# Where the odd slot of a pair of attention steps stands among TensorE's instructions

## The chip, the cores and the metric

The kernel runs on one core of a Trainium2 chip. The metric is device time in microseconds (us): the median of three executions of the kernel before is 1056.26 us (1056.03 to 1058.4).

## What is computed

A perceiver block: cross-attention of 256 latent rows over 4096 context rows (batch 4, width 256, 16 heads of 16), then a causal linear attention over the latents with exponential features, then a gated feed-forward. Each is added to `x` after a layer norm. Cut to what matters:

```python
Q = layernorm(x) @ Wq.T + bq; K = ctx @ Wk.T + bk; V = ctx @ Wv.T + bv     # per head: 16 columns
x = x + softmax(Q K^T / 4) V @ Wh.T + bh                                   # 256 x 4096 scores, 16 heads, 4 batches
qf, kf = exp(clip(norm(q) @ omega*sqrt(2s) - s)); A = causal(qf kf^T)      # the linear attention, per head
x = x + (A v / (A 1)) @ Wout + bout
x = x + (silu(h @ wg.T) * (h @ wu.T)) @ wd.T                               # h = layernorm(x), integer weights
```

## The kernel before, in words

The context of a batch is cut into 8 chunks of 512 rows; the loop calls them passes, p0 to p7. A pass has 16 steps. One step is 128 context rows (one of four tiles) times 4 heads. Its scores are 4 matmuls into one of the two score tiles `ps_s` (line 711), ScalarE takes their exponential into one of four `probs` tiles (line 975), and its values product is 4 fp32 matmuls (8 instructions) of 17 columns each, side by side in four column strips of the array, added up in `ps_o` (line 700). The values product lags its scores by two steps.

While a pass attends, TensorE also projects the chunks to come, through the one bank `ps_p`: the values of the next chunk, tile 0 to 3, in steps 1, 3, 5 and 7 (V0 to V3, line 546, 6 matmuls), and the keys of the chunk after it in steps 9 and 12 (K0 and K1, line 538, 6 matmuls). Most of these steps are odd. VectorE takes each result out of `ps_p` (V: line 1034; K: lines 1012 to 1019), and the next projection waits for that (`v_ready`, `k_out`).

Everything else of the block is spread over the steps of a later batch as named stages. A tail stage belongs to the batch before (`oT0`, `wh`, `ln1T`, `feat0` to `feat7`, `A0` to `A15`, `pv0` to `pv3`, `gu0` to `gu5`, `down` and so on), a head stage to the batch after (`ln0`, `ln0T`, `q`, `kbd`, `max0` to `max3`, `maxT`). Batches are counted 0 to 3: batch 0 carries only head stages, batches 1 and 2 both, batch 3 only tail stages, and the tail of batch 3 runs alone at the end. The table `AT` gives a tail stage its step, `HEAD_AT` a head stage. All products of stages go through the one bank `ps_a`, so `stage` on TensorE waits until VectorE has finished the stage whose product stood there before (`ready`, semaphore `operand`). Some stages (`ln0`, `kbd`, `o`, `gate0` to `gate5`) are on VectorE alone.

What a step carries beside its attention (a projection and the stages that fall on it) is its slot. `fast_slot(b, p, s)` on TensorE issues the slot's projection first and then its stages. VectorE has a `fast_slot` of its own that takes the same things in the same order, slot by slot. One wait there matters below: before V0 of a pass is copied to its buffer (`fast_values_out`), VectorE waits until all values products that read that buffer are done (`pv_done`); the last two of them are issued in steps 0 and 1 of the same pass.

TensorE handles two steps at a time (a pair: s even, s + 1). Written S for the two steps' scores (8 matmuls), E for the even slot, O for the two values products of the pair before (16 instructions), D for the odd slot, a pair is S E O D. The score tile of a step is free again when the exponential of the step two before has been taken.

Of the kernel before, what the change touches and what calls it, by code (L numbers as in the profile page):

```python
# [209 lines left out]
def perceiver(nc, x, ctxT, wqT, bq, wkT, bk, wvT, bv, whT, bh, wqkv, bqkv, wout, bout,  # L210
              omega, nodes, weights, wgT, wuT, wdT, out):
    ctx = ExitStack()
    with ctx:
# [116 lines left out]
        def head_of(b):  # L330
            return (b, b - 1, False)
# [4 lines left out]
        def stages_at(b, step):  # L336

            return [(n, tail_of(of) if n in TAIL else head_of(of)) for of, n in stages_of(b, step)]
# [188 lines left out]
        def _(pe):  # L527
# [22 lines left out]
            def project_keys(c, q, j):  # L550

                pe.wait_ge(c["ctx_split"], q + 1)
                if j:
                    pe.wait_ge(c["k_out"], q * 2 + 1)
                elif q:
                    pe.wait_ge(c["v_ready"], q * TT)
                for part in range(CI):
                    project(c, ("k", j, part), q, q % 2)

            def project_values(c, q, tile):  # L560

                if tile:
                    pe.wait_ge(c["v_ready"], q * TT + tile)
                else:
                    pe.wait_ge(c["k_out"], q * 2 + 2)
                project(c, ("v", tile, 0), q, q % 2)
# [117 lines left out]
            def products(c, names, clock, alone=False):  # L684
                for name in names:
                    if alone and name[:4] == "gate" and name != "gate0":

                        down_part(c, int(name[4:]) - 1, ps_a, clock)
                    if name not in VECTOR_ONLY:
                        stage(c, name, clock, alone)  # L690
# [43 lines left out]
            def fast_scores(b, q, s):  # L734

                n = q * STEPS + s
                if n >= LAG:
                    pe.wait_ge(fast["exp_done"], n - LAG + 1)
                score(fast, s, q % 2, qstacks[b % 2])

            def fast_values(n):

                b, q, s = n // BS, n // STEPS, n % STEPS
                if b and n % BS == 0:
                    pe.wait_ge(fast["operand"], fast.at("operand", tail_of(b - 1), "o"))
                value_product(fast, n, s, q % 2, q % NCH == 0, q % NCH == NCH - 1, q * TT + s // G)

            def fast_slot(b, p, s):

                q = b * NCH + p  # L750
                if s in VALUE_SLOTS and q + 1 < B * NCH:
                    project_values(fast, q + 1, VALUE_SLOTS[s])
                if s in KEY_SLOTS and q + 2 < B * NCH:
                    project_keys(fast, q + 2, KEY_SLOTS[s])
                for name, clock in stages_at(b, p * STEPS + s):
                    products(fast, [name], clock)
# [19 lines left out]
            for b in range(B):  # L776
                for p in range(NCH):
                    q = b * NCH + p
                    if p == 0:
                        pe.wait_ge(fast["q_stacked"], (b + 1) * Q_STACKED)  # L780
                        pe.wait_ge(fast["operand"], fast.at("operand", head_of(b), "maxT"))
                    if p == 0 and b == 1:
                        pe.wait_ge(late_in, 16 * 15)
                        pe.wait_ge(w_ready, 1)
                    pe.wait_ge(fast["k_stacked"][p % 2], (q // 2 + 1) * STACKED)
                    for s in range(0, STEPS, LAG):
                        for t in range(LAG):
                            fast_scores(b, q, s + t)
                        fast_slot(b, p, s)
                        if q or s:  # L790
                            for t in range(LAG):
                                fast_values(q * STEPS + s + t - LAG)
                        fast_slot(b, p, s + 1)
            for t in range(LAG):
                fast_values(B * BS + t - LAG)
            products(fast, TAIL[:NORMALISED], tail_of(B - 1), True)
# [597 lines left out]
```

## Time and profile before

| | |
|---|---|
| median of 3 executions | 1056.26 us |
| the profiled execution | 1058.43 us, its span 1056.3 us |
| TensorE matmul busy | 943.5 us, 89% of the span |
| VectorE, ScalarE, GpSimd busy | 566.0, 548.6, 113.6 us |
| first scores | 45.4 us |
| batch 0, 1, 2, 3 of the loop | from 45.4, 238.4, 479.0, 721.4 us; the loop ends at about 935 us |
| last tail, alone | about 935 to 1056.3 us |

The matmul rows of a trace are pipelined: a matmul is listed as longer than the distance to the next one. The distance between the starts of two rows tells what a piece of the order costs, and so the start of a pair's first score matmul to that of the next pair is the length of a pair. A batch has 64 pairs. "Idle before <- releaser" names the last event that an instruction waited for.

### The profile page before, as it was taken

To read this page: it belongs to the slowest core of one execution; us is meant where nothing else is said; L and a number is where in the kernel's file an instruction comes from. 1 tells how busy PE (TensorE), PEld (TensorE's weight loads), DVE (VectorE), ACT (ScalarE), POOL (GpSimd) and SP (SyncE) were. 2 spreads that over 40 slices of the span, in tenths; PEclk is the share of its full clock that TensorE was granted. 3 is DMA by queue.
4 is the path that set the end of the run, shared out by engine and by line. 5 is a ranking of instruction groups with operands and counts; after the bars stand their busy time and mean duration, and the time that the engine had idled before them with its cause. 6 is when DMAs were issued, how large, how long until landed. Compare 5 with 4: busy or idle time off the path is not lost.

```text
span 1056.3 us, 20657 instructions
## 1 busy us (share of the span) xinstructions
PE 943.5 (89%) x8586; PEld 621.2 (59%) x8595; DVE 566.0 (54%) x1009; ACT 548.6 (52%) x595; POOL 113.6 (11%) x137
## 2 busy tenths in 40 slices
PE   4689999999999998799999998979999999955765
PEld 3456665656666665566666765556566666632544
DVE  7633335565555457745654557645555556514546
ACT  5157666667466555446465555536565655820101
POOL 1700000000311100000221000000131100003300
PEclk9799999999999999999999999989999999986887
DMA  4997665587555555257655554266655543110000
GB/s 137 212 216 137 136 130 110 120 159 158 105 111 96 110 110 111 65 91 143 132 107 111 110 106 96 65 110 138 123 110 111 102 90 72 30 41 0 1 1 12
DMA packets 65219, 108.94 MB, mean 103 GB/s; under 512 B 21537, under 2 KB 52641, under 8 KB 61665
## 3 DMA queue, kind: packets, MB, share of 16 engines
q1 hardware_dynamic: 63328, 103.17, 47.6%
q0 software_dynamic: 1792, 4.40, 1.7%
q8 instruction: 70, 1.15, 0.5%
q14 instruction: 29, 0.23, 0.1%
HBM read 78.71 MB, written 28.84 MB: 102 GB/s over the span
## 4 chain that ended last, share of the span: by engine, by line
PE 68%; DVE 12%; issue 7%; ACT 4%; DMA 4%; POOL 2%; DVEq 2%; SPq 0%; POOLq 0%
PE ps_o L700 17%; PE ps_s L711 17%; PE ps_p L546 9%; PE ps_p L538 9%; ACT probs L975 4%; DVE kfeat L1207 2%; PE ps_a L654 2%; PE ps_a L680 2%; PE ps_a L648 2%; PE ps_a L593 2%; DMA kstack<-kscr 2%; PE ps_a L667 1%; PE ps_a L637 1%; POOL rnorm L878 1%; PE ps_a L655 1%
## 5 line engine op out<-in xcount | busy, mean ns | idle before, releaser
L975 ACT ACTIVATE probs<-ps_s 128x1024 f32<-128x1024 f32 x512 | 497.2, 1022 | 384.3 <-PE ps_s L711 383.3
L711 PE MATMUL ps_s<-qstack,kstack 128*128 128x256 bf16 x2048 | 277.0, 276 | 24.1 <-DVE ksample L1116 8.8
L700 PE MATMUL ps_o<-probs,values 128*17 128x256 f32 x4096 | 274.9, 385 | 0.0
L711 PEld LDWEIGHTS ps_s<-qstack,kstack 128*128 128x128 bf16 x2048 | 184.3, 99 | 93.2 <-issue 43.0
L700 PEld LDWEIGHTS ps_o<-probs,values 128*17 128x17 f32 x4096 | 96.2, 97 | 109.9 <-issue 38.9
L1034 DVE TENSOR_TENSOR values<-ps_p,bv_sb 128x256 f32<-128x256 f32 x128 | 54.2, 423 | 145.1 <-PE ps_p L546 145.0
L1012 DVE TENSOR_SCALAR kparts<-ps_p,b_heads 128x512 bf16<-128x512 f32 x64 | 48.1, 751 | 102.1 <-PE ps_p L538 101.8
L546 PE MATMUL ps_p<-wv_hi,ctx_hi 128*128 128x256 f32 x256 | 86.8, 339 | 10.7 <-DVE values L1034 5.8
L546 PEld LDWEIGHTS ps_p<-wv_hi,ctx_hi 128*128 128x128 f32 x256 | 49.2, 192 | 66.2 <-issue 50.2
L546 PE MATMUL ps_p<-wv_hi,ctx_lo 128*128 128x256 f32 x256 | 73.1, 285 | 0.0
L546 PE MATMUL ps_p<-wv_lo,ctx_hi 128*128 128x256 f32 x256 | 72.9, 285 | 0.0
L538 PE MATMUL ps_p<-ctx_hi,wk_hi 128*128 128x512 f32 x128 | 57.6, 450 | 7.9 <-DVE values L1034 3.5
L881 POOL TENSOR_TENSOR rstd<-veps,half_power 128x2 f32<-128x2 f32 x12 | 8.4, 696 | 507.2 <-DVE veps L1047 507.2
L911 POOL TENSOR_TENSOR kfeat<-feat,half_mask 128x256 f32<-128x256 f32 x64 | 37.9, 613 | 227.8 <-ACT feat L952 227.8
L952 ACT ACTIVATE feat<-feat,node_neg 128x512 f32<-128x512 f32 x32 | 23.1, 722 | 68.7 <-DVE feat L1191 68.7
L538 PE MATMUL ps_p<-ctx_hi,wk_lo 128*128 128x512 f32 x128 | 51.6, 403 | 0.0
L538 PE MATMUL ps_p<-ctx_lo,wk_hi 128*128 128x512 f32 x128 | 51.4, 401 | 0.0
L1014 DVE SCALAR_TENSOR_TENSOR krest<-ps_p,b_heads,kparts 128x512 f32<-128x512 f32 x64 | 48.1, 751 | 5.1 <-issue 0.4
L546 PEld LDWEIGHTS ps_p<-wv_hi,ctx_lo 128*128 128x128 f32 x256 | 49.7, 194 | 0.0
L546 PEld LDWEIGHTS ps_p<-wv_lo,ctx_hi 128*128 128x128 f32 x256 | 49.5, 193 | 0.0
L878 POOL TENSOR_TENSOR rnorm<-ss,half_power 128x32 f32<-128x32 f32 x8 | 43.9, 5502 | 38.1 <-DVE ss L1178 38.1
L1019 DVE TENSOR_TENSOR kparts<-krest,kparts 128x512 bf16<-128x512 f32 x64 | 44.3, 692 | 5.6 <-issue 0.9
(214 smaller groups left out, 998.7 us busy)
## 6 DMA issues: line engine op xcount, KB each, us to landing
kscr<-kparts SPq DMA_DIRECT2D x64, 384.0 KB, 2.6
kstack<-kscr SPq DMA_DIRECT2D x32, 768.0 KB, 7.8
ctx_raw<-ctxT SPq DMA_DIRECT2D x32, 512.0 KB, 13.2
kstack<-kscr SPq DMA_DIRECT2D x32, 512.0 KB, 10.4
kstack<-kscr SPq DMA_DIRECT2D x32, 256.0 KB, 11.7
qstack<-qscr SPq DMA_DIRECT2D x16, 128.0 KB, 4.4
qscr<-qparts SPq DMA_DIRECT2D x4, 384.0 KB, 3.3
xh<-x SPq DMA_DIRECT2D x4, 256.0 KB, 13.6
```

What stands on the lines that cost most here:

```text
L538: last = mm(ps_p[:, :], w[:, k, j * P:(j + 1) * P], a[:, k, :], start=(k == 0 and n == 0), stop=(k == CI - 1 and n == 2))
L546: last = mm(ps_p[:, 0:D], a[:, k, j * P:(j + 1) * P], w[:, k, :], start=(k == 0 and n == 0), stop=(k == CI - 1 and n == 2))
L700: last = mm(ps_o[32 * j:32 * j + DH + 1, g * S:(g + 1) * S], values[par][:, i, g * GH + j, :], probs[s % NPROB][:, j * S:(j + 1) * S], sta ...
L711: last = mm(ps_s[s % 2][:, j * S:(j + 1) * S], kstack[par][:, u, i * P:(i + 1) * P], queries[:, u, :], start=True, stop=True)
L878: pool.tensor_tensor(rnorm[:, n, :], ss[:, n, :], half_power[:, n, :], ALU.pow).then_inc(c["powered"], 1)
L911: pool.tensor_tensor(kfeat[:, p % 2, k, :], feat[:, p % 2, 1, :], half_mask[:, k:k + 1].to_broadcast([P, S]), ALU.mult).then_inc(c["kfeat" ...
L952: nc.scalar.activation(feat[:, p % 2, :, :], feat[:, p % 2, :, :], ACT.Exp, bias=node_neg[:, :]).then_inc(c["acted"], 1)
L975: nc.scalar.activation(probs[n % NPROB][:, :], ps_s[n % 2][:, :], ACT.Exp, scale=float(DH) ** -0.5).then_inc(fast["exp_done"], 1)
L1012: v.tensor_scalar(kparts[:, 0, j, :], ps_p[:, :], bias, None, ALU.add)
L1014: v.scalar_tensor_tensor(krest[:, :], ps_p[:, :], bias, kparts[:, 0, j, :], ALU.add, ALU.subtract).then_inc(c["k_out"], 1)
L1019: v.tensor_tensor(kparts[:, 2, j, :], krest[:, :], kparts[:, 1, j, :], ALU.subtract).then_inc(c["k_parts"], 1)
L1034: v.tensor_tensor(values[q % 2][:, tile, :, 0:DH], ps_p[:, 0:D].rearrange("p (h d) -> p h d", h=H), bv_sb[:, :].rearrange("p (h d) -> p h ...
```

## The change

In the loop over pairs, TensorE issues the odd slot right behind the even one, ahead of the two values products. The pair S E O D becomes S E D O. Nothing is added or removed, and the lists of instructions of VectorE, ScalarE, GpSimd and the DMA queue stay as they are.

```diff
@@ -787,10 +787,10 @@
                         for t in range(LAG):
                             fast_scores(b, q, s + t)
                         fast_slot(b, p, s)
+                        fast_slot(b, p, s + 1)
                         if q or s:
                             for t in range(LAG):
                                 fast_values(q * STEPS + s + t - LAG)
-                        fast_slot(b, p, s + 1)
```

TensorE in batch 1, pass 3, steps 6 and 7, before. Line 655 ends stage `A4` (even slot), line 700 is the values product, line 546 is V3 and the last row begins stage `A5` (odd slot):

```order
L655 MATMUL ps_a<-feat,kfeat 128x128
L700 MATMUL ps_o<-probs,values 17x256 [waits f_v_ready,f_exp_done]
L700 MATMUL ps_o<-probs,values 17x256 x3
L700 MATMUL ps_o<-probs,values 17x256 [waits f_exp_done]
L700 MATMUL ps_o<-probs,values 17x256 x3
L546 MATMUL ps_p<-wv_hi,ctx_hi 128x256 [waits f_v_ready]
L546 MATMUL ps_p<-wv_hi,ctx_lo 128x256
L546 MATMUL ps_p<-wv_lo,ctx_hi 128x256
L546 MATMUL ps_p<-wv_hi,ctx_hi 128x256
L546 MATMUL ps_p<-wv_hi,ctx_lo 128x256
L546 MATMUL ps_p<-wv_lo,ctx_hi 128x256
L654 MATMUL ps_a<-feat,kfeat 128x256 [waits f_kfeat,f_operand]
```

The same place of TensorE now:

```order
L655 MATMUL ps_a<-feat,kfeat 128x128
L546 MATMUL ps_p<-wv_hi,ctx_hi 128x256 [waits f_v_ready]
L546 MATMUL ps_p<-wv_hi,ctx_lo 128x256
L546 MATMUL ps_p<-wv_lo,ctx_hi 128x256
L546 MATMUL ps_p<-wv_hi,ctx_hi 128x256
L546 MATMUL ps_p<-wv_hi,ctx_lo 128x256
L546 MATMUL ps_p<-wv_lo,ctx_hi 128x256
L654 MATMUL ps_a<-feat,kfeat 128x256 [waits f_kfeat,f_operand]
L655 MATMUL ps_a<-feat,kfeat 128x128
L700 MATMUL ps_o<-probs,values 17x256 [waits f_v_ready,f_exp_done]
L700 MATMUL ps_o<-probs,values 17x256 x3
L700 MATMUL ps_o<-probs,values 17x256 [waits f_exp_done]
```

Between the end of `A4` and the start of `A5`, which waits for VectorE's copy of `A4` (`f_operand`), there stood a values product and V3; now V3 alone stands there. The values product follows `A5`.

TensorE at the start of a pass (batch 1, pass 3, steps 0 and 1), before: the end of `feat2`, the values product, V0 (its first row waits for `f_k_out`), then `A2`:

```order
L648 MATMUL ps_a<-qkT,om_sb 128x256
L700 MATMUL ps_o<-probs,values 17x256 [waits f_exp_done]
L700 MATMUL ps_o<-probs,values 17x256 x3
L700 MATMUL ps_o<-probs,values 17x256 [waits f_exp_done]
L700 MATMUL ps_o<-probs,values 17x256 x3
L546 MATMUL ps_p<-wv_hi,ctx_hi 128x256 [waits f_k_out]
```

The same place of TensorE now, from V0's last matmul on:

```order
L546 MATMUL ps_p<-wv_lo,ctx_hi 128x256
L654 MATMUL ps_a<-feat,kfeat 128x256 [waits f_kfeat,f_operand]
L655 MATMUL ps_a<-feat,kfeat 128x128
L700 MATMUL ps_o<-probs,values 17x256 [waits f_exp_done]
L700 MATMUL ps_o<-probs,values 17x256 x3
L700 MATMUL ps_o<-probs,values 17x256 [waits f_exp_done]
L700 MATMUL ps_o<-probs,values 17x256 x3
```

VectorE at this place, before and now alike (the copies of `feat2`, V0, `A2` and `A3`, and V1):

```order
L1191 TENSOR_SCALAR feat<-ps_a,clip_most,clip_least 128x512 [waits f_product]
L1034 TENSOR_TENSOR values<-ps_p,bv_sb 128x16x16 [waits f_pv_done,f_v_proj]
L1195 TENSOR_TENSOR amat<-ps_a,causal 128x384 [waits f_product] x2
L1034 TENSOR_TENSOR values<-ps_p,bv_sb 128x16x16 [waits f_v_proj]
L1197 COPY qk<-ps_a 128x256 [waits f_product]
```

The values product that V0's copy waits for (`f_pv_done`) was issued before V0; now it is issued behind V0 and `A2`.

## Rows read from the trace of the kernel before

**Rows 1.** The page: busy time of each engine, its share, instructions.

```profile
PE 943.5 (89%) x8586; PEld 621.2 (59%) x8595; DVE 566.0 (54%) x1009; ACT 548.6 (52%) x595; POOL 113.6 (11%) x137
```

**Rows 2.** Batch 3: us; PE, PEld, DVE, ACT, POOL busy (count); PE clock, DMA share, GB/s.

```profile
721.40:935.00 213.60, 212.19 (x2063) 140.06 (x2060) 111.54 (x198) 131.44 (x147) 21.88 (x20) 1.00 0.46 97
```

**Rows 3.** Waits of PE in batch 1: us in total, times, longest.

```profile
PE ps_s L711 <- DVE ksample L1116: 4.1, 1, 4.1
PE ps_a L585 <- DVE amat L1201: 2.3, 1, 2.3
```

**Rows 4.** Timeline of PE, pairs with V3, K0, and K1: start, length, what.

```profile
128.04 1.05 PE L711 MATMUL ps_s<-qstack,kstack 128*128 128x256 bf16 x8
...
130.82 1.05 PE L711 MATMUL ps_s<-qstack,kstack 128*128 128x256 bf16 x8
...
134.30 1.05 PE L711 MATMUL ps_s<-qstack,kstack 128*128 128x256 bf16 x8
...
372.58 1.04 PE L711 MATMUL ps_s<-qstack,kstack 128*128 128x256 bf16 x8
...
375.94 0.61 PE L711 MATMUL ps_s<-qstack,kstack 128*128 128x256 bf16 x4
```

**Rows 5.** Timeline of PE, batch 1, pass 3, steps 6 and 7.

```profile
332.28 0.38 PE L655 MATMUL ps_a<-feat,kfeat 128*128 128x128 f32 x2
332.60 1.06 PE L700 MATMUL ps_o<-probs,values 128*17 128x256 f32 x16
333.59 0.38 PE L546 MATMUL ps_p<-wv_hi,ctx_hi 128*128 128x256 f32 x1
...
334.40 0.59 PE L654 MATMUL ps_a<-feat,kfeat 128*128 128x256 f32 x2
334.83 0.38 PE L655 MATMUL ps_a<-feat,kfeat 128*128 128x128 f32 x2
335.05 0.82 PE L711 MATMUL ps_s<-qstack,kstack 128*128 128x256 bf16 x6
```

**Rows 6.** Timeline of DVE at that place: the copy of A4.

```profile
332.70 0.56 DVE L1195 TENSOR_TENSOR amat<-ps_a,causal 128x384 f32<-128x384 f32 x1 [1.12 <-PE ps_a L655]
```

**Rows 7.** Timeline, batch 1, pass 4, steps 0 to 2: `feat5`, its copy, `A8`.

```profile
351.59 1.03 PE L648 MATMUL ps_a<-qkT,om_sb 128*128 128x256 f32 x4
352.65 0.81 DVE L1191 TENSOR_SCALAR feat<-ps_a,clip_most,clip_least 128x512 f32<-128x512 f32 x1 [0.44 <-PE ps_a L648]
...
353.52 0.70 PE L654 MATMUL ps_a<-feat,kfeat 128*128 128x256 f32 x2
```

**Rows 8.** Timeline, start of batch 2: the copy `o`, `oT0` and its copy.

```profile
481.37 1.23 DVE L1154 COPY qk<-ps_o 128x1024 f32<-128x1024 f32 x1
...
482.91 0.60 PE L624 MATMUL ps_a<-ident,qk 128*128 128x128 f32 x4
...
484.53 0.42 DVE L1072 TENSOR_TENSOR y<-ps_a,rden 128x256 f32<-128x256 f32 x1
```

**Rows 9.** Timeline, batch 1, pass 1: chain of `wh`, copy of V1, then V2.

```profile
268.12 0.69 DVE L1162 TENSOR_TENSOR xs<-xs,ps_a 128x512 f32<-128x512 f32 x1 [1.49 <-PE ps_a L593]
...
271.66 0.42 DVE L1034 TENSOR_TENSOR values<-ps_p,bv_sb 128x256 f32<-128x256 f32 x1
272.13 0.39 PE L546 MATMUL ps_p<-wv_hi,ctx_hi 128*128 128x256 f32 x1 [0.28 <-DVE values L1034]
```

**Rows 10.** PE in batch 1, pass 5: K0 behind the chain of `wout`.

```profile
397.69 0.47 PE L538 MATMUL ps_p<-ctx_hi,wk_hi 128*128 128x512 f32 x1 [0.37 <-DVE values L1034]
```

**Rows 11.** PE in batch 0, pass 5: V1 behind the set-up on DVE.

```profile
171.26 0.39 PE L546 MATMUL ps_p<-wv_hi,ctx_hi 128*128 128x256 f32 x1 [2.00 <-DVE values L1034]
```

**Rows 12.** DVE in batch 1: the copy of `gu0`; `kbd`.

```profile
408.23 0.42 DVE L1201 TENSOR_TENSOR amat<-kfeat,ps_a 128x256 f32<-128x256 f32 x1 [0.91 <-ACT kfeat L959]
...
446.98 1.29 DVE L1116 TENSOR_TENSOR ksample<-kparts,head_mask 128x512 bf16<-128x512 bf16 x2
```

**Rows 13.** The stretch behind `max0` in batch 1 (columns as in Rows 2).

```profile
448.50:453.10 4.60, 4.54 (x32) 2.89 (x31) 1.22 (x3) 2.60 (x4) 0.00 (x0) 0.63 1.22 189
```

## The prediction, as it was made

> **What bounds the kernel now.** I read the page first, then the waits of PE batch by batch, then the timeline of PE pair by pair. PE is busy for 89% of the span, the next engine for 54% [rows 1], and in the stretch of batch 3, where no head stages run, PE is busy for 212.2 of 213.6 us at full clock [rows 2]. So in the loop, 890 of the 1056 us, the time is the length of TensorE's list, pair after pair. Two things can lengthen or shorten it: what it costs to pass from one kind of matmul to the next, and waits, of which there are few now. In batch 1 the two largest are 4.1 us for `kbd` (it is `max0` that waits, its record is missing and the wait is booked on the next scores) and 2.3 us for `gu1`'s copy ahead of `ln0T` [rows 3]. The other engines keep their lists, so all that can change is when TensorE gets to its instructions.
>
> **Part 1, the seams get cheaper.** A pair with K0 in its odd slot (S O D) takes 134.30 - 130.82 = 3.48 us; a pair with K1 in its even slot, which already has the order S E O, takes 375.94 - 372.58 = 3.36 us [rows 4]. Same work, same clock: the order S D O is 0.12 us shorter than S O D. The V pair has the same two seams (128.04 to 130.82, 2.78 us [rows 4]); I take 0.11 us for both. There are 124 V's and 30 K0's in the loop, so this part is worth at most 154 x 0.11 = 17 us.
>
> By the Trainium skill (TensorEngine Tiling (Array Packing), Key Properties) changing the tiling mode, and not just the tile, drains TensorE. The values product is the only one in column strips beside `pv`, and a plain pair enters and leaves it once in either order, so by that rule alone this part would be worth nothing, and the sum below would come out some 12 us higher, 1085 us: slower still. The two rows of K pairs say 0.12 us; I go by them.
>
> **Part 2, the copies of neighbours are no longer covered.** All stages share one bank. Where the even and the odd slot of a pair both have a stage, the odd one waits for VectorE's copy of the even one. Before, a values product and a projection stood between; now the projection alone. From the last matmul of `A4` (the second of the x2 at 332.28, 0.11 us later) to `A5` at 334.40 there were 2.0 us [rows 5]; without the values product (332.60 to 333.59, 0.99 us) and with cheaper seams 0.82 us are left. What is needed is the product's end, the copy and its release:
> - `A`: last matmul 332.39, copy from 332.70 for 0.56 [rows 5, 6], release 0.06: 0.93 us. A stall of 0.11 cancels the saving of the seam: 0.0 for `A4`/`A5`, `A8`/`A9`, `A14`/`A15`. Where a `pv` follows (`A3`, `A11`) it then stands beside the values product with no change of strips between: I take -0.3 each, and for `pv1` and `pv3`, which stood beside it before and now don't, +0.3 each. Bounds for these four: from -0.3 to +0.5 each.
> - `feat`: last matmul 352.24 (351.59 and three of 0.216), copy from 352.65 for 0.81, next stage 353.52 [rows 7]: 1.28 us, a stall of 0.46, less the seam 0.1 and a little for the wider exit: +0.27, three times (`feat0`/`feat1`, `feat2`/`A2`, `feat6`/`A10`).
> - `oT0`/`oT1`: last matmul 483.23 (482.91 and three of 0.108), the copy's last part ends at 484.95 [rows 8]: 1.78 us, +0.87. `o2T1`/`y2T` has the same copy without the check of the denominators, some 0.4 us less: +0.45. `ln1T`/`qk0`, a plain copy: +0.15.
>
> Sum per tail: 0.8 + 0.9 + 0.45 + 0.15 = 2.3 us, thirteen neighbours.
>
> **Part 3, long chains that end in an odd slot.** After `wh` (even) VectorE has a layer norm from 268.12 on, only then copies V1 at 271.66, and V2 waits until 272.13 [rows 9]. V2's time is set by `wh`, not by what TensorE does between. Before, two values products ran ahead of V2, now one, and the second comes behind it: the wait grows from 0.35 us by a whole values product with its seams, 0.99 [rows 5] + 0.1, and the savings of V1 and V2 are lost in it. Net +1.1. K0 behind `wout` is the same [rows 10]: +1.1. In batches 1 and 2 `ln0T` and `max0` are such places as well: VectorE goes without a pause of note from the copy of `gu0` (408.23) to that of `gu1`, and from the copy of `gu4` to `kbd` at 446.98 [rows 3, 12]. Also once V1 behind the set-up in batch 0 [rows 11], and in batch 0 `ln0T` and `max0`, which wait there too. Each +1.1. If such a chain's start came earlier by as much as the values product, it would be 0; each is bounded by 0 and +1.3.
>
> **Part 4, V0's copy waits for the values product behind it.** VectorE stops at V0's copy until that product is done, then takes V0's copy (0.42) and that of the odd stage in the same slot. From `A2`'s last matmul: product 0.88, its release 0.37, V0 0.42, copy 0.56, release, 2.35 us with the gaps between, against 2.07 us until `A3` asks: +0.3. With the copies' lengths of the others: `yT`/`wh` +0.4, `feat5`/`A8` +0.5, `A15`/`pv3` +0.15. Per tail +1.35. In the plain passes only V1 could wait, 0.26 us are spare, so nothing. In the first pair of a tail batch the copy `o` (1.23 us [rows 8]) starts later as well, since the product that it waits for does, and `oT0` waits for it: +0.5 (with the seam lost 0 to 0.9). `max0`'s copy in batches 1 and 2: +0.3.
>
> **Part 5, old waits of even slots go.** A stage in an even slot now has a values product more behind the odd one ahead of it. `A8` came 0.19 us late behind `feat5` [rows 7] and `o2T1` 0.38 behind `o2T0`; those outside pass starts sum to -0.9 per tail, and `maxT` gets 0.3 back and `gu5` 0.15 in a batch with a head.
>
> **The sum.** A tail batch, passes 0 to 5: 2.3 (part 2) + 2.2 (part 3) + 1.35 + 0.5 (part 4) - 0.9 (part 5) - 13 x 0.11 (slots left over with the plain saving) = +4.0; three of them +12.1. Passes 6 and 7 of batches 1 and 2: 2 x 1.1 + 0.3 - 0.5 - 3 x 0.11 = +1.7 each, +3.4. Batch 0: 3 x 1.1 - 30 x 0.11 - 0.3 = -0.3 (pass 0 waits for its keys, so its savings are lost). Passes 6 and 7 of batch 3: -0.4. Start and the last tail: unchanged. Total +14.8 us.
>
> **The clock.** Behind the wait for `kbd` TensorE runs for a while at a mean granted clock of 0.63 of full, that is partly at 1.2 GHz and not 2.4 [rows 13]: 4.6 x 0.37 = 1.7 us of work lost there. The waits ahead of `ln0T` and `max0` grow to 3.4 and 5.2 us. I add 0.75 us in each of the two batches, as part of what the clock takes is taken from waits that follow: +1.5.
>
> The profiled execution took 1058.43 us for a span of 1056.3; the median of the runs is 1056.26, 0.2% less. The sum of 16.3 us makes a span of 1072.6 and that profiled execution 1074.7; on the level of the median, 1072.6 us.
>
> **Rivals.**
> A, the seams win: faster. If VectorE's copies were on time in the odd slots (for instance because a stage's product is ready for VectorE earlier than the next one's asking shows), part 1 stays alone: 149 slots x 0.11 = 16 us less, 1040 us. It decides as soon as parts 2 to 4 together stay under 16 us instead of some 31. Against it: the lengths of copies are read, not guessed, and 0.82 us hold neither 1.28 nor 1.78. Rows 2 speaks for it only so far as PE has almost no idle time that could be taken away otherwise.
> B, it comes out even: the stalls of the odd slots are repaid by waits that vanish in even slots and by the seams; within 3 us of 1056. In batch 3 there is 213.6 - 212.2 = 1.4 us of idle time to repay with [rows 2], too little for a stretch that I expect to grow by 4.
> C, the clock falls often: if the new waits of 1.4 to 1.8 us (V2, K0, three batches) and those ahead of `ln0T` each brought a time at 1.2 GHz, some eight more at 1.2 to 1.7 us [rows 13], it would be 1072.6 + 8 x 1.5 = 1085 us. Against it: 2.3 us of wait ahead of `ln0T` in batch 1 [rows 3] let the clock stand there.
>
> The Trainium skill (TensorE: Matmul & The Clock Gate, Why this matters for your kernels) advises against idle gaps of more than about 3 us between bursts of matmuls; by it the wait ahead of `ln0T`, now 3.4 us, becomes a risk and those of 1.8 us don't, which is C in its small form and inside my range. No row shows what the clock does after a wait of 3.4 us.
>
> **How the numbers follow.** Mine 0.73, C 0.13, A 0.06, B 0.08. The measurement of this kernel tells no change from one below 0.3%, 3 us. Parts 2 to 4 carry the doubt: all of them at two thirds, 1062; at their upper bounds, 1082; with C's tail 1085. Range 1061 to 1084. Faster 0.06, same 0.08, slower 0.86.
>
> **What would show it.** A plain V pair of batch 0 at 2.67 us and the K0 pair at 3.36 (part 1). `oT1`, `feat1`, `A2`, `A10` behind a stall of PE for VectorE of 0.3 to 0.95 us, and V2 at 1.7 us in place of 0.35 (parts 2 and 3). The copy of V0 waiting for line 700 in place of line 546 (part 4). Batch 3 longer by some 3.6 us, batches 1 and 2 by 6.5 with the clock, batch 0 the same. I am wrong in part 1 if the V pair stays at 2.78, and in the rest if batch 3 gets shorter.

## The result, and the profile after

The changed kernel takes 1075.86 us (median of 4, 1072.89 to 1077.19) against 1056.99 for the kernel before in the same comparison: ratio 1.0174, 95% interval 1.0157 to 1.019. On the level of the earlier median of 1056.26 us that is 1074.6 us, where 1072.6 was forecast and 1061 to 1084 was the range. The profiled execution took 1075.62 us, its span is 1073.6 against 1056.3: +17.3 where +16.3 was the sum.

The busy time of every engine is what it was, within 3.1 us. The page of the changed kernel:

```profile
PE 943.2 (88%) x8595; PEld 623.6 (58%) x8595; DVE 562.9 (52%) x1009; ACT 548.7 (51%) x595; POOL 113.6 (11%) x137
```

So the 17 us are idle time of TensorE. Batch 3 shows it with no clock in play. The row that answers to [rows 2], of the changed kernel (same columns; it ends at the start of the last pair, 0.3 us earlier in the order than that of [rows 2]):

```profile
734.10:951.20 217.10, 210.74 (x2060) 139.87 (x2056) 110.38 (x198) 131.16 (x147) 21.91 (x20) 1.00 0.46 95
```

Up to the same pair the kernel before takes 213.22 us and is busy for 211.81 of them. So TensorE's busy time is 1.1 us less, at the same full clock, and idle time went from 1.4 to 6.4 us: the stretch is 3.9 us longer. Less busy time is the cheaper seams, the idle time is the waits. These are the waits of TensorE in that stretch, after (who waited for whom, us in total, times, longest):

```profile
PE ps_p L538 <- DVE values L1034: 1.5, 1, 1.5
PE ps_p L546 <- DVE values L1034: 1.4, 1, 1.4
PE ps_a L624 <- DVE y L1072: 0.8, 1, 0.8
PE ps_a L654 <- DVE feat L1191: 0.7, 3, 0.4
PE ps_a L585 <- DVE y L1072: 0.4, 1, 0.4
PE ps_a L624 <- DVE qk L1154: 0.4, 1, 0.4
PE ps_a L593 <- DVE xT L1101: 0.2, 1, 0.2
PE ps_a L648 <- DVE feat L1191: 0.2, 1, 0.2
```

Line by line these are K0 behind `wout`, V2 behind `wh`, `oT1` behind `oT0`, then `A2`, `A8` and `A10` behind a `feat` (0.19, 0.35 and 0.20 us; `A8`'s is part 4's, behind V0's late copy), `y2T` behind `o2T1`, `oT0` behind `o`, `wh` behind `yT`, and `feat1` behind `feat0`: the places that the prediction named.

**The seams.** The same pair as the first one of [rows 4] (batch 0, pass 3, V3), and the K0 pair behind it, timeline of PE after:

```profile
122.57 1.05 PE L711 MATMUL ps_s<-qstack,kstack 128*128 128x256 bf16 x8
123.38 0.36 PE L546 MATMUL ps_p<-wv_hi,ctx_hi 128*128 128x256 f32 x1
...
124.26 1.06 PE L700 MATMUL ps_o<-probs,values 128*17 128x256 f32 x16
125.25 1.05 PE L711 MATMUL ps_s<-qstack,kstack 128*128 128x256 bf16 x8
126.06 0.48 PE L538 MATMUL ps_p<-ctx_hi,wk_hi 128*128 128x512 f32 x1
...
128.62 0.28 PE L711 MATMUL ps_s<-qstack,kstack 128*128 128x256 bf16 x1
```

The V pair takes 125.25 - 122.57 = 2.68 us (2.78 before), the K0 pair 3.37 (3.48 before).

**The neighbours.** Timeline at `A4`/`A5`, after, the place of [rows 5]:

```profile
332.08 0.38 PE L655 MATMUL ps_a<-feat,kfeat 128*128 128x128 f32 x2
332.22 0.36 PE L546 MATMUL ps_p<-wv_hi,ctx_hi 128*128 128x256 f32 x1
...
333.11 0.70 PE L654 MATMUL ps_a<-feat,kfeat 128*128 128x256 f32 x2
```

From `A4`'s end block at 332.08 to `A5` it is now 1.03 us, where it was 2.12; the values product follows. Timeline at `feat6`/`A10`, after, where the copy does not fit:

```profile
359.12 0.81 DVE L1191 TENSOR_SCALAR feat<-ps_a,clip_most,clip_least 128x512 f32<-128x512 f32 x1 [2.28 <-PE ps_a L648]
...
359.51 0.28 PE L546 MATMUL ps_p<-wv_lo,ctx_hi 128*128 128x256 f32 x1
...
359.99 0.70 PE L654 MATMUL ps_a<-feat,kfeat 128*128 128x256 f32 x2 [0.20 <-DVE feat L1191]
```

V2's last matmul starts at 359.51, and V2's matmuls are 0.12 us apart, so that `A10` could have gone at about 359.63; it goes at 359.99, 0.06 us after the copy of `feat6` ends.

**V0's copy.** Timeline at the start of pass 3, after, the piece of order shown ahead of the prediction:

```profile
321.52 0.38 PE L655 MATMUL ps_a<-feat,kfeat 128*128 128x128 f32 x2
321.83 1.06 PE L700 MATMUL ps_o<-probs,values 128*17 128x256 f32 x16
...
323.03 0.42 DVE L1034 TENSOR_TENSOR values<-ps_p,bv_sb 128x256 f32<-128x256 f32 x1 [2.10 <-PE ps_o L700]
323.37 0.55 DVE L1195 TENSOR_TENSOR amat<-ps_a,causal 128x384 f32<-128x384 f32 x1
```

The copy of V0, whose last matmul started at 320.50, waits until 323.03 for line 700, and `A2`'s copy stands behind it.

### The profile page after: what moved, and what is told of

It reads as the page before. It is cut to its first block, busy times and chain, and to the rows that moved or that the text cites. A ratio compares the mean times of both kernels' runs of the same rounds, so it can differ in the third digit from the quotient of the medians.

```text
span 1073.6 us, 20666 instructions
## 1 busy us (share of the span) xinstructions
PE 943.2 (88%) x8595; PEld 623.6 (58%) x8595; DVE 562.9 (52%) x1009; ACT 548.7 (51%) x595; POOL 113.6 (11%) x137
## 4 chain that ended last, share of the span: by engine, by line
PE 66%; DVE 14%; issue 6%; ACT 4%; DMA 3%; DVEq 2%; POOL 2%; SPq 0%; POOLq 0%
PE ps_o L700 18%; PE ps_s L711 17%; PE ps_p L538 8%; PE ps_p L546 6%; ACT probs L975 4%; PE ps_a L654 2%; DVE kfeat L1207 2%; PE ps_a L648 2%; PE ps_a L680 2%; PE ps_a L593 2%; DMA kstack<-kscr 1%; DVE feat L1191 1%; PE ps_a L637 1%; POOL rnorm L878 1%; PE ps_a L655 1%
## 5 line engine op out<-in xcount | busy, mean ns | idle before, releaser
L711 PE MATMUL ps_s<-qstack,kstack 128*128 128x256 bf16 x2048 | 280.1, 278 | 6.8 <-DMA qstack<-qscr 3.8
L711 PEld LDWEIGHTS ps_s<-qstack,kstack 128*128 128x128 bf16 x2048 | 178.7, 99 | 145.8 <-issue 80.8
L538 PE MATMUL ps_p<-ctx_hi,wk_lo 128*128 128x512 f32 x128 | 51.1, 400 | 0.0
```

The lines of the kernel that those rows point to most:

```text
L538: last = mm(ps_p[:, :], w[:, k, j * P:(j + 1) * P], a[:, k, :], start=(k == 0 and n == 0), stop=(k == CI - 1 and n == 2))
L711: last = mm(ps_s[s % 2][:, j * S:(j + 1) * S], kstack[par][:, u, i * P:(i + 1) * P], queries[:, u, :], start=True, stop=True)
```

## The experiments

In each comparison the kernel before ran on the same chip. `early(b, p, s)` decides for each pair whether the odd slot comes ahead of the values products (as in the changed kernel) or behind them (as before):

```diff
                         fast_slot(b, p, s)
-                        fast_slot(b, p, s + 1)
+                        if early(b, p, s):
+                            fast_slot(b, p, s + 1)
                         if q or s:
                             for t in range(LAG):
                                 fast_values(q * STEPS + s + t - LAG)
+                        if not early(b, p, s):
+                            fast_slot(b, p, s + 1)
```

My theory is that of the prediction: cheaper seams, uncovered copies, chains that end in odd slots, V0's late copy. The rivals were that the loss is spread over all moved slots, and that the seams only look cheaper.

**e1_neighbours**, the pairs in which both slots hold a stage:

```diff
+NEIGHBOURS = {(0, 2), (1, 6), (2, 6), (3, 0), (3, 2), (3, 6), (4, 0), (4, 2), (4, 4), (4, 6), (5, 0), (5, 2), (5, 4)}
+def early(b, p, s):
+    return b > 0 and (p, s) in NEIGHBOURS
```

> The odd slot stands ahead of the values products only in the thirteen pairs of a tail batch in which both slots hold a stage (39 of 256 pairs). Theory (uncovered copies of VectorE): about +8 us against the kernel before (2.3 of part 2, 1.0 of V0's late copy, less old waits), all of it in these pairs and the ones right behind, +1.0 in pass 0 step 2 (oT0/oT1), -0.3 where a pv follows in the odd slot. Rival (the loss is spread over all moved slots, by the clock or by ScalarE being asked later): 17 x 39/154 = +4 us, and the same in each pair.

Measured: ratio 1.0093 (1.007 to 1.0116), +9.8 us. Passes 0 to 5 of batch 3, first the kernel before, then e1 (stretches as in [rows 2]):

```profile
721.46:890.92 169.46, 168.30 (x1612) 111.56 (x1609) 91.99 (x169) 99.61 (x107) 21.88 (x20) 1.00 0.52 107
```

```profile
729.26:901.66 172.40, 169.07 (x1612) 111.50 (x1608) 91.33 (x169) 99.63 (x107) 21.94 (x20) 1.00 0.51 105
```

+2.94 us in this stretch at full clock, and +2.9 in the same stretch of batches 1 and 2. From the starts of the score blocks, pair by pair: `oT0`/`oT1` +0.91, `ln1T`/`qk0` +0.24, `feat0`/`feat1` +0.36, `A11`/`pv2` -0.33, all others as in the changed kernel within 0.02 us. (In the changed kernel `feat0`/`feat1` is only +0.19: there the pair before it is moved too, and in e4, where that one alone is moved, `feat0`'s pair is 0.17 us shorter.) In passes 0 to 5 pairs that kept their order kept their length, but for those right behind a moved one. The spread rival, with equal shares of 0.1 us per slot, is out.

**e2_chains**, six pairs of 256:

```diff
+CHAIN_ENDS = {(1, 4), (5, 8)}
+def early(b, p, s):
+    return b > 0 and (p, s) in CHAIN_ENDS
```

> The odd slot stands ahead only in pass 1 step 4 (V2 behind the chain of wh) and pass 5 step 8 (K0 behind the chain of wout) of batches 1 to 3, six pairs of 256. Theory (a chain of VectorE that ends in an odd slot costs one whole values product with its seams): 6 x 1.1 = +6.6 us. Rival (loss spread over all moved slots): 17 x 6/154 = +0.7 us.

Measured: ratio 1.0073 (1.0046 to 1.01), +7.7 us. The six pairs are longer by 1.07 to 1.10 us each, and no other pair of those stretches moves by more than 0.02. V2 behind the chain of `wh` in e2 (timeline of PE; the line number is shifted by the edit), to set against [rows 9]:

```profile
269.80 1.05 PE L718 MATMUL ps_s<-qstack,kstack 128*128 128x256 bf16 x8
272.12 0.39 PE L553 MATMUL ps_p<-wv_hi,ctx_hi 128*128 128x256 f32 x1 [1.27 <-DVE values L1044]
```

V2 starts at 272.12, before at 272.13, behind a chain that starts at 268.10 here and at 268.12 there (the addition behind `wh`): the chain sets it. The values product that had used this time now comes behind V2. The six pairs make 6.5 us of the 6.8 by which the profiled span grew; the interval of the ratio is +4.9 to +10.6 us.

**e3_three_buffers**, the changed kernel with a third buffer, so that V0's copy has nothing to wait for (the declaration of the third buffer and its ones column are left out here):

```diff
-                value_product(fast, n, s, q % 2, q % NCH == 0, q % NCH == NCH - 1, q * TT + s // G)
+                value_product(fast, n, s, q % 3, q % NCH == 0, q % NCH == NCH - 1, q * TT + s // G)
-                if tile == 0 and q >= 2:
-                    dve.wait_ge(fast["pv_done"], (q - 1) * STEPS)
-                v.tensor_tensor(values[q % 2][:, tile, :, 0:DH],
+                if tile == 0 and q >= 3:
+                    dve.wait_ge(fast["pv_done"], (q - 2) * STEPS)
+                v.tensor_tensor(values[q % 3][:, tile, :, 0:DH],
```

> The changed kernel with three buffers for the projected values in place of two, so that the copy of V0 need not wait for the values products that are now behind it. Theory: the 1.35 us of part 4 per tail batch go, and 0.3 at max0 in batches 1 and 2: 4 to 5 us less than the changed kernel, +12 to +13 against before; A3, A8, pv3 and wh start earlier. The stall of oT0 behind the copy o stays. Rival (V0's late copy is covered as in the plain passes): no change against the changed kernel, +17.

Measured: ratio 1.0125 (1.0101 to 1.0149), +13.2 us against before and 5.2 less than the changed kernel. Pair by pair against the changed kernel, in each of the batches 1 to 3: pass 1 step 2 (`wh`) -0.50, pass 3 step 2 (`A3`) -0.37, pass 4 step 2 (`A8`) -0.62, pass 5 step 2 (`pv3`) -0.17, and no other pair of passes 0 to 5 by more than 0.02. That is 1.66 us per tail. The copy of `A2` in e3, which was at 323.37 behind V0's copy, now follows its product (`A2`'s last block at 318.78):

```profile
318.11 0.41 DVE L1034 TENSOR_TENSOR values<-ps_p,bv_sb 128x256 f32<-128x256 f32 x1
...
319.20 0.56 DVE L1195 TENSOR_TENSOR amat<-ps_a,causal 128x384 f32<-128x384 f32 x1 [0.68 <-PE ps_a L655]
```

A thing that I had not expected: `ln0T` of batch 0 comes 1.2 us sooner too, and passes 6 and 7 of batch 0 take 50.1 us in place of 52.8. The pair behind it is 1.4 us shorter as well, since the clock doesn't fall there in e3. See the next section.

**e4_mixed**, the odd slot ahead only where the odd slot loses nothing by it: where nothing in it hangs on the even slot or on the pass start, and in two pairs where a `pv` follows an `A` whose copy fits under the projection:

```diff
+TAIL_EARLY = {(0, 4), (0, 6), (0, 8), (1, 8), (2, 0), (2, 2), (2, 4), (2, 8), (3, 2), (3, 4), (3, 8), (4, 6), (4, 8)}
+def early(b, p, s):
+    if b == 0:
+        return (p, s) not in {(5, 2), (6, 2), (7, 0)}
+    if b == B - 1 and p == 6:
+        return True
+    return (p, s) in TAIL_EARLY or (b < B - 1 and p == 7 and s in (6, 8))
```

> The odd slot stands ahead only where no stage or projection of the odd slot waits for the even one and no pass start delays a copy: all pairs of batch 0 but three, 13 pairs of each tail batch (two of them pv), pass 6 of batch 3, two head pairs. Theory (the seams are 0.1 us cheaper, 0.3 where pv meets the values product): 32 x 0.105 + 3 x 1.75 + 0.9 + 0.4 = -10 us against before, ratio 0.9905. Rival (seams only look cheaper, the modelled start of a matmul moves): 0 within 1 us. Rival (loss spread over moved slots): 81 of 154 slots, +9 us.

Measured: 1046.61 us, ratio 0.9902 (0.988 to 0.9923), 10.4 us faster than the kernel before and the fastest of all versions. Batch 3, passes 0 to 5, in e4:

```profile
711.07:878.58 167.51, 166.34 (x1612) 111.88 (x1609) 92.17 (x169) 99.62 (x107) 21.78 (x20) 1.00 0.53 108
```

TensorE is busy for 2.0 us less than before (168.30) and idle for the same 1.2 us: the seams are real time and not a matter of how a start is drawn. The two `pv` pairs among them get 0.30 us shorter each. In the first (pass 3, step 2) `pv0` and the values product now stand side by side, 0.21 us from block to block (319.37 to 319.58), where line 661 and the next scores were 0.36 apart (326.96 to 327.32) in the kernel before. Batch 0 is 5.2 us shorter; not all of it is seams (see the clock, below). The two blocks of pass 3, step 2 in e4:

```profile
319.37 0.42 PE L673 MATMUL ps_a<-amat,v 128*32 128x128 f32 x8
319.58 1.07 PE L712 MATMUL ps_o<-probs,values 128*17 128x256 f32 x16
```

**e5_passes_0_to_5**, the order of before in passes 6 and 7 of batches 0 to 2:

```diff
+def early(b, p, s):
+    return p < 6 or b == B - 1
```

> The changed order in passes 0 to 5 of batches 0 to 2 and in all of batch 3; in passes 6 and 7 of batches 0 to 2, where ln0T and max0 wait for long chains, the order of before. Theory: the 9.9 us that passes 6 and 7 of these batches gained in the changed kernel go (3.0, 4.1 and 2.9), of which some 5 are the clock; the granted clock falls no oftener behind ln0T and max0 than before; +7.4 us against before, ratio 1.007. Rival (the clock falls because of the many small stalls of the passes ahead): the drops stay and the time stays above +11 us.

Measured: ratio 1.009 (1.0061 to 1.0119), +9.5 us, its profiled span +6.5. The interval, +6.4 to +12.6 us, holds both the +7.4 of the theory and the +11 of the rival; the stretches decide. Passes 0 to 5 of batches 1 to 3 take 173.5 us as in the changed kernel, passes 6 and 7 take 49.8, 71.6 and 71.9 us, as before (49.8, 71.1, 73.0). So that part of the loss sits in passes 6 and 7, and behind `ln0T` the clock fell in neither batch, with the small stalls of passes 0 to 5 all there: the rival falls for these places. In pass 5 of batch 0 the clock fell once more than before, behind the wait for the set-up, and that pass is longer by 2.35 us, not by 0.76 as in the changed kernel. That is not the order: e1 and e6, with the order of before in that pass, have the same fall and are 1.55 us longer there than the profile of before.

**e6_three_buffers_before**, the control: the kernel before with the three buffers of e3.

> Control: the kernel before with three buffers for the projected values. Theory: in the order of before the copy of V0 finds its values products done, so the third buffer changes nothing: 0 within 1 us, and every pair from pass 2 on as long as before. Rival (a third buffer helps by itself, e3 says nothing on the order): 3 to 5 us less.

Measured: ratio 1.0005 (0.9989 to 1.0021), and passes 0 to 5 of batch 3 take 169.48 us (169.46 before). The third buffer does nothing by itself; e3 is an effect of the order. This run also shows what the clock does with no change of order. Passes 6 and 7 of batch 1, first the kernel before, then e6:

```profile
407.90:479.01 71.11, 59.94 (x541) 40.38 (x541) 46.16 (x77) 33.62 (x43) 0.70 (x1) 0.98 0.49 99
```

```profile
407.32:480.12 72.80, 62.55 (x544) 41.65 (x541) 46.28 (x77) 33.60 (x43) 0.70 (x1) 0.93 0.48 96
```

Same instructions, mean granted clock 0.93 in place of 0.98, 1.7 us longer.

## Why the prediction came out right, step by step

Lengths are from score block to score block of the profiled executions, 1056.3 and 1073.6 us.

| stretch | forecast | measured |
|---|---|---|
| up to the first scores | 0 | -2.0 |
| batch 0 | -0.3 | -0.4 |
| batches 1 to 3, passes 0 to 5 | 12.1 | 4.1, 4.1, 4.1 |
| batches 1 and 2, passes 6 and 7 | 3.4 + 1.5 for the clock | 4.1 and 2.9 |
| batch 3, passes 6 and 7 | -0.4 | -0.2 |
| last tail, alone | 0 | +0.7 |
| sum | 16.3 | 17.3 |

**How near the sum came** is in part luck, in two places. The first scores came at 45.4 us in the profile of before and between 43.3 and 45.2 us in the seven others, whatever the order, so the -2.0 us is scatter and not the change. And in batch 0 two errors cancel. Split by pass, the prediction's terms come to about -1.7 us for passes 0 to 5 and +1.4 for 6 and 7; measured were -3.4 and +3.0. Both differences are for the most part falls of the clock that the sum did not have: one that went and one that came (below).

**What bounds the kernel**: right. Only TensorE's list changed, and the loop is as long as that list with its waits.

**Part 1, the seams**: right. 0.10 us for a V, 0.11 for a K0, pair for pair, in the changed kernel and in e4; 0.30 to 0.33 where a `pv` comes to stand beside the values product. Where it comes from, from the start of one block's last matmul to the start of the next block (medians of passes 0 to 5, batches 1 to 3): before, scores to values product 0.20 us, values product to V 0.31, V to scores 0.12; after, scores to V 0.03, V to values product 0.21, values product to scores 0.31. The way into the column strips and the way out cost the same in both orders; what changes is that V to scores costs 0.12 and scores to V 0.03, 0.09 of the 0.10 us. By the drain at a change of tiling mode alone (the Trainium skill, TensorEngine Tiling (Array Packing), Key Properties) a plain pair should have gained nothing; the runs decide against that reading. For the `pv` pairs, where the number of changes of mode does drop, the rule and the 0.2 us that these gain beyond a plain pair agree. The K1 pair of the prediction's comparison was well chosen: in batch 0 a K1 pair takes 3.60 us, as its scores are held by the exponentials (block of 1.28 us at 136.26 and not 1.05), and such a pair would have seemed to speak against the saving.

**Part 2, the neighbours**: right in kind and in sum. Single terms were off by up to 0.11 us: `A` pairs +0.11 where 0 was put, `feat0` +0.36 for 0.27, `pv1` +0.22 for 0.3, `ln1T` +0.24 for 0.15. In e1, with the thirteen pairs alone, the stretch grew by 2.9 us, V0's late copies in three of them included.

**Part 3, the chains**: right for `wh` and `wout`, 1.07 to 1.10 us each for 1.1, shown by e2 with nothing else moved, for the set-up of batch 0 (V1's pair +1.17) and for `max0` of batch 0 (+1.08). V2's wait is 1.4 us, as the sum of part 3 gives it; the 1.7 in the prediction's list of signs did not follow from that sum. `max0`'s pair in batches 1 and 2 is 9.17 us, against 7.20 in the order of before with the clock down as well: +1.97 where 1.1 + 0.3 was put. What makes up that difference is open.

The attribution was wrong for `ln0T` of batch 0. I put it among chains that start in an even slot. There is no `gu1` in batch 0; the chain starts at V0's copy, in the odd slot, and would have come earlier together with V0, if that copy had not had to wait for the values product. e3 takes that wait away, and `ln0T`'s pair is then as long as before (4.13 us, 5.34 in the changed kernel). It was part 4's mechanism with part 3's price (+1.22 for 1.1). In batches 1 and 2 `ln0T` stays late in e3, so there it is the chain from `gu0`.

**Part 4, V0's copy**: right, a little undersized. 1.66 us per tail by e3 where 1.35 was put; `oT0` behind `o` +0.6 (1.50 in the changed kernel less 0.91 in e1) for 0.5.

**Part 5**: right in size. The pairs behind `ln1T`/`qk0` and behind `o2T1`/`y2T` are each 0.17 us shorter in e1 without being moved, `feat0`'s pair 0.17 in e4, and `o2T1`'s own pair is +0.07 where the stall alone was put at +0.45: together 0.9.

**The clock**: the weak step. I put 0.75 us in each of batches 1 and 2, on a wait ahead of `ln0T` that had grown to 3.4 us in one piece. It came in two pieces, 1.06 us ahead of V1 and then, as before, 2.3 us ahead of `ln0T`. And I took it from batch 1 of the kernel before that the clock stands behind 2.3 us [rows 3]. Batch 2 of the same trace has the same wait, and 0.3 us behind it the granted clock was 0.50. Timeline of PE before, then the stretch (columns as in [rows 2]):

```profile
657.53 0.66 PE L585 MATMUL ps_a<-ident,xh 128*128 128x128 f32 x3 [2.32 <-DVE amat L1201]
```

```profile
657.83:661.24 3.41, 3.41 (x24) 1.86 (x26) 3.07 (x4) 1.94 (x2) 0.00 (x0) 0.50 0.86 129
```

In the order of before the clock fell behind `ln0T` in 7 of 12 places (batches 1 and 2 of before, e1, e2, e4, e5 and e6), and pass 6 then took 34.7 to 34.8 us and not 33.6. In the changed order (the changed kernel and e3) it fell in 4 of 4. Whether the change makes falls there likelier is not shown by so few. In four places of the loop the changed kernel's clock fell where it had not in the profile of before, or for longer, one of them in batch 0 (pass 6, behind a wait of 1.9 us, where the pair of step 4 grew by 1.33 us instead of shrinking by 0.1), which I had at nothing.

The passes 6 and 7 of the changed kernel grew by 4.1 and 2.9 us against the single profile of before. Against e6 (72.8 us in both) it is 2.4 and 3.0, and against the mean of the five profiles that have the order of before there (71.1 to 73.1 us, mean 72.4) it is 2.8 and 3.4. How much of the 17 us is due to the clock stays open by some 2 us.

What the clock gave back in passes 0 and 1 of batch 0 does come with the order. In the four profiles with the order of before in these passes (before, e1, e2, e6) TensorE waits 3.1 to 4.1 us for its keys ahead of pass 1, the clock is at half there, and the two passes take 51.1 to 53.0 us. In the four with the new order (the changed kernel, e3, e4, e5) it waits sooner, 1.9 to 2.8 us ahead of V1 in pass 0, and 1.0 us or less ahead of pass 1; the clock does not fall in pass 1, and the two passes take 48.8 to 49.6 us. About 1 us of the difference is seams. The prediction had the savings of pass 0 as lost and this at nothing.

**The rivals.** A (the seams win, 1040) fell, since parts 2 to 4 cost more than 16 us; e4 shows that it is what is left when these are avoided, 1046.6 us. B fell on batch 3: +3.9 us there at full clock. C fell in its larger part: waits of 1.4 and 1.5 us (V2, K0) brought no fall of the clock in any of the three batches. Its smaller part, a fall behind `ln0T`, came true in batches 0, 1 and 2 of the changed kernel, though in batch 2 it had fallen there before as well.

## What to carry to other kernels

When one engine's list is the bound and another engine copies its products out of a single bank, a block of independent work between two dependent products is worth the copy's length; moved by one place it no longer covers that copy, though the work is the same and the other lists don't change. Look per place at what must fit between (product end, copy, release) against what stands there, and move only where it fits: a table of exceptions turned +1.7% into -1.0% here. And check which buffers a later copy frees itself from: an instruction that waits in order on the copying engine holds up all copies behind it.

## What the runs showed of the hardware

- The order of kinds of matmul costs time with equal work: scores, projection, values product is 0.10 to 0.11 us shorter per pair than scores, values product, projection, and two column-strip blocks side by side save 0.2 us more.
- With no fall of the clock the pairs repeat very closely: passes 0 to 5 of batches 1, 2 and 3 took 169.46, 169.49 and 169.46 us before and 173.55, 173.54 and 173.57 after. A difference of 0.05 us in one pair can be read from a single profile, where the whole time scatters by 2 us and more.
- The granted clock fell to half in different places in executions of the same order: behind the same wait of 2.3 us ahead of `ln0T` it stood in batch 1 of the kernel before and fell in its batch 2, and in both batches of e6. The fall made pass 6 1.1 us longer.
